# GpSimd adds the identity to two blocks of the loaded slab, in place of TensorE's identity products

## The reference

```python
R = S + eye(N)                     # S is adj
R = R / R.sum(-1)
for n in range(2):                 # two steps
    A  = top_p_attention(Xa, W1, W2, W3)   # softmax over 2048 keys, cut to the top 90% of the mass
    Xf = R @ Xf                    # propagation
    Xa = A @ Xa                    # attention
    Z  = Z + Xf @ U1[n].T + Xa @ U2[n].T
```

## Time and profile before

| | us |
|---|---|
| median of 3 runs | 1008.23 |
| their range | 1007.75 to 1008.57 |
| the profiled execution's own time | 1006.43 |
| its span, first to last instruction | 1004.6 |
| busy: PE, DVE, ACT, POOL | 804.8, 666.2, 474.7, 68.8 |

### The profile page before, as it was taken

How to read it: one execution, slowest core, us unless ns; L and a number is a source line. 1 busy time by engine, 2 the same in 40 slices (tenths; PEclk the granted TensorE clock), 3 DMA queues, 4 the chain that set the end, 5 groups by cost and what they waited for, 6 DMA issues and landing times.

```text
span 1004.6 us, 11941 instructions
## 1 busy us (share of the span) xinstructions
PE 804.8 (80%) x3886; PEld 551.0 (55%) x3886; DVE 666.2 (66%) x2092; ACT 474.7 (47%) x945; POOL 68.8 (7%) x63
## 2 busy tenths in 40 slices
PE   4879984988888865786898788685598999994994
PEld 4844432756666654683575565565295585542342
DVE  5967858488777689734979876788596022245715
ACT  4886334336545556344435646846944241024111
POOL 0020001010000000000000000201001000013001
PEclk9889986988988996989897888899799999997898
DMA  9849502543103100000253300601342819100001
GB/s 336 331 165 432 214 10 84 168 167 126 44 1 125 44 1 2 1 2 0 84 175 117 128 1 1 226 1 53 130 172 70 321 41 427 63 1 0 1 0 42
DMA packets 20219, 108.23 MB, mean 108 GB/s; under 512 B 1824, under 2 KB 8752, under 8 KB 9776
## 3 DMA queue, kind: packets, MB, share of 16 engines
q1 hardware_dynamic: 18752, 106.77, 28.6%
q10 hardware_dynamic: 1392, 0.61, 0.3%
HBM read 88.23 MB, written 19.14 MB: 107 GB/s over the span
## 4 chain that ended last, share of the span: by engine, by line
PE 49%; DVE 25%; ACT 12%; issue 9%; DMA 2%; POOL 1%; DVEq 1%; POOLq 0%; SPq 0%; ACTq 0%
PE PS L802 9%; PE PS L671 6%; DVE AT L1518 6%; PE PS L607 6%; PE PS L541 5%; PE PS L724 4%; PE PS L871 4%; DVE mxv L1657 4%; ACT BC L1243 3%; DVE nd L1521 3%; PE PS L1052 3%; PE PS L1028 3%; ACT AT L1243 3%; DVE AT L2100 3%; PE PS L1058 2%
## 5 line engine op out<-in xcount | busy, mean ns | idle before, releaser
L1074 ACT ACTIVATE AT<-PS 128x512 f32<-128x512 f32 (+2 forms) x240 | 118.7, 559 | 121.3 <-PE PS L541 86.8
L541 PE MATMUL PS<-ident,AT 128*128 128x128 f32 x544 | 85.8, 293 | 38.5 <-DVE rS L2169 18.9
L1657 DVE TENSOR_REDUCE mxv<-PS 128x1 f32<-128x2048 f32 x32 | 73.2, 2288 | 56.7 <-PE PS L724 56.6
L724 PE MATMUL PS<-K,ST 64*128 64x512 f32 x256 | 87.9, 779 | 13.6 <-ACT EA L1211 7.7
L541 PEld LDWEIGHTS PS<-ident,AT 128*128 128x128 f32 x544 | 69.0, 152 | 46.9 <-DVE rS L2169 20.1
L2100 DVE MAX8 AT<-AT 128x8 f32<-128x256 f32 (+2 forms) x336 | 92.7, 347 | 0.7
L802 PE MATMUL PS<-AT 128*128 128x128 f32 x512 | 72.1, 291 | 13.1 <-ACT AT L1074 12.6
L802 PE MATMUL PS<-hr,AT 128*128 128x128 f32 x512 | 71.3, 289 | 8.2 <-ACT AT L1074 7.4
L802 PEld LDWEIGHTS PS<-AT 128*128 128x128 f32 x512 | 65.7, 202 | 21.9 <-ACT AT L1074 17.7
L802 PEld LDWEIGHTS PS<-hr,AT 128*128 128x128 f32 x512 | 65.0, 200 | 17.3 <-ACT AT L1074 11.2
L1074 ACT ACTIVATE ST<-PS 128x512 f32<-128x512 f32 (+3 forms) x43 | 23.9, 561 | 104.6 <-PE PS L1058 24.3
(11 more groups left out here) (297 smaller groups left out, 1370.5 us busy)
## 6 DMA issues: line engine op xcount, KB each, us to landing
AT<-keep_at SPq DMA_DIRECT2D x32, 1024.0 KB, 5.0
EA<-in_adj SPq DMA_DIRECT2D x20, 1024.0 KB, 6.5
keep_at<-AT SPq DMA_DIRECT2D x8, 2048.0 KB, 25.0
AT<-keep_at SPq DMA_DIRECT2D x8, 2048.0 KB, 12.4
AT<-in_adj SPq DMA_DIRECT2D x12, 1024.0 KB, 6.6
EA<-keep_degrees SPq DMA_DIRECT2D x1, 1024.0 KB, 6.5
keep_x<-K SPq DMA_DIRECT2D x4, 256.0 KB, 6.8
out<-EA SPq DMA_DIRECT2D x4, 256.0 KB, 2.3
```

The source lines that it names most:

```text
L541: return pe.transpose(dst, src, ident[0:p, 0:p])
L724: return pe.matmul(bank(to + n), ST[1][half_rows, k * P:(k + 1) * P], keys[half_rows, n * BK:(n + 1) * BK], start=True, stop=True)
L1074: return act.activation(dst, src, ACT.Copy)
L1657: v(dve.tensor_reduce(mxv[:, odd:odd + 1], PS[:, b:b + 4, :], AX.XY, ALU.max))
```

## The change

GpSimd now adds the identity into the slab in SBUF, once it has been loaded: one instruction on two blocks of 128x128, the diagonal blocks of the unit's own two tiles. TensorE's two identity products go. Within each half PE now takes the unit's own tiles (`2*c` and `2*c + 1`, in the first half for `c` below 4, in the second otherwise) last, and waits for a new semaphore `slab_own` ahead of them. POOL does the adds behind the square root of a group: units 0 to 3 behind the root of group 0, 4 and 5 behind that of group 1, 6 and 7 behind that of group 2, and the same in step 1.

```diff
+            def slab_added(u):
+
+                c = u % UNITS
+                pool.wait_ge(slab_in[2 * c // HALF], 16 * (u + 1))
+                here = slab[:, 2 * c:2 * c + 2, :].rearrange("p j (k c) -> p (j k) c", c=P)[:, 0:4:3, :]
+                pool.tensor_tensor(here, here, ident[:, :].unsqueeze(1).to_broadcast([P, 2, P]), ALU.add)\
+                    .then_inc(slab_own, 1)
+
+            SLABS = {0: range(0, 4), 1: range(4, 6), 2: range(6, UNITS),
+                     4: range(UNITS, UNITS + 4), 5: range(UNITS + 4, UNITS + 6), 6: range(UNITS + 6, 2 * UNITS)}
             for gi in range(STEPS * NB):
...
                 pool.tensor_tensor(sZ[:, gi % 2, :], Z[:, gi % 2, :], ex[:, 1, 0:G], ALU.pow).then_inc(root_ok, 1)
+                for u in SLABS.get(gi, ()):
+                    slab_added(u)
...
                 left = hr if p == 0 else Xf
-                for j in range(NT):
-                    if j % HALF == 0:
-                        pe.wait_ge(slab_in[j // HALF], 16 * (u + 1))
-                    mm = pe.matmul(bank(6)[:, 2 * P:4 * P], left[:, j, :], slab[:, j, :],
-                                   start=(j == 0), stop=(j == NT - 1))
-                    if j == HALF - 1:
-                        mm.then_inc(un_half, 1)
-                    if j == 0:
-                        for k in range(2):
-                            pe.matmul(bank(6)[:, (2 + k) * P:(3 + k) * P], left[:, 2 * c + k, :], ident[:, :],
-                                      start=False, stop=False)
-                mm.then_inc(un_half, 1)
+                own = (2 * c, 2 * c + 1)
+                for h in range(2):
+                    pe.wait_ge(slab_in[h], 16 * (u + 1))
+                    tiles = [j for j in range(h * HALF, (h + 1) * HALF) if j not in own]
+                    tiles += [j for j in own if j // HALF == h]
+                    for j in tiles:
+                        if j == own[0]:
+                            pe.wait_ge(slab_own, u + 1)
+                        mm = pe.matmul(bank(6)[:, 2 * P:4 * P], left[:, j, :], slab[:, j, :],
+                                       start=(h == 0 and j == tiles[0]), stop=(h == 1 and j == tiles[-1]))
+                    mm.then_inc(un_half, 1)
```

More of the change, by code:

```diff
@@ L244, in gnn_kernel @@
             sure_steps ksum_ok mean_mm mean_ok lnz_ok gap_ok guess_steps guess_ok
-            cs_ok at_saved un_half un_st un_t un_row un_pr un_z th_ok sum_ok roots_ok fin_sq bias_ok h2_t h2_st hw_mm x2_ok mask_ok
+            cs_ok at_saved un_half slab_own un_st un_t un_row un_pr un_z th_ok sum_ok roots_ok fin_sq bias_ok h2_t h2_st hw_mm x2_ok mask_ok
             ln_steps ln_sq ln_var ln_pow ln_root ln_y ln_t ln_ts ln_x ln_x2 h2_act diag_ok early_in x2_dma"""
@@ L254, in gnn_kernel @@
          ksum_ok, mean_mm, mean_ok, lnz_ok, gap_ok, guess_steps, guess_ok,
-         cs_ok, at_saved, un_half, un_st, un_t, un_row, un_pr, un_z, th_ok, sum_ok, roots_ok, fin_sq, bias_ok, h2_t, h2_st, hw_mm, x2_ok, mask_ok,
+         cs_ok, at_saved, un_half, slab_own, un_st, un_t, un_row, un_pr, un_z, th_ok, sum_ok, roots_ok, fin_sq, bias_ok, h2_t, h2_st, hw_mm, x2_ok, mask_ok,
          ln_steps, ln_sq, ln_var, ln_pow, ln_root, ln_y, ln_t, ln_ts, ln_x, ln_x2, h2_act, diag_ok, early_in, x2_dma) = [sem(n) for n in names.split()]
```

## The result

The changed kernel takes 1002.61 us, the median of 12 runs (995.95 to 1006.02). The kernel before, run beside it, takes 1008.04 us (12 runs, 1003.70 to 1009.15). The ratio is 0.994 with a 95% interval of 0.9916 to 0.9963.

What follows compares the result with a forecast made beforehand. TensorE was taken to bound the kernel only where it ends last, in eight of 16 units. 3.56 us gained less 0.95 of contention gave 2.6 us, so a median of 1005.6 us, range 1003.8 to 1007.8.

Steps and rivals of the forecast that it cites:

- PE's work pays, and only on the chain: TensorE, busy 80% of the span: removing matmuls pays only where PE ends last, in eight of 16 units.
- The rival that all 16 count: Propagation units: all 16 gain as if PE bound everywhere, 7.1 us less contention, 1002.1 us; chance 0.02.
- The chain units are worth 8 x 0.445 = 3.56 us: Units 0, 1, 2, 4, 5, 7, 9, 10: removed products save their high-clock price, 3.56 us; other end 4.37.
- Low price saved in full: Products at the low clock save their full price, small DVE operations get past: 4.0 us, 1004.2 us; chance 0.14.
- What is late next: Where stalls shrink: DVE takes units 0 to 2's gain whole, unit 5's refill moves up, ACT still ends last at 314.54.
- The reordering costs nothing: Diagonal tiles last in their half: moves nothing by itself, cost nothing, bounds -0.1 and +0.1 us.
- PE never waits for POOL: Adds before the diagonal tiles: POOL has 3.2 to 4.2 us, PE waits nothing; at most 1.5 us for one unit.
- An add takes 0.6 us: POOL's add on two blocks: between 0.6 and 2.4 us, taken as 0.6.
- the slower rival: DVE before units 0, 4 and after POOL's step 1 root: 2.4 us adds hold DVE, 3.6 us slower, 1011.9; chance 0.07.
- Contention of 0.38 + 0.38 + 0.19: Adds of units 0, 4 and, by half, 8 delay DVE work on the chain: 0.95 us in all.
- The forecast of the median: Whole kernel: profiled 1003.8 us plus the 1.8 us by which the median exceeded the profiled execution gives 1005.6 us.

Runs made afterwards that it cites:

- matched pair: The traces of the kernel before and of g, side by side, alike up to unit 0; spans 1004.6 and 998.3 us.
- e1: Kernel before without any identity product and without adds, so the identity is missing; 995.87 us (six runs, ratio 0.9895), repeated 1001.32 us (0.9948).
- g: g_chain_only: kernel before without identity products in units 0, 1, 2, 4, 5, 7, 9, 10, no adds; 1000.70 us, 0.994; repeated 1002.32 us.
- h: h_pool_off_path: changed kernel, but units 0, 4, 8 keep PE's identity products and get no add; 999.72 us (0.9944), repeated 1000.60 us (0.9936).
- fill_chain_only: g plus 20 unread identity-by-itself products in PE's waits in the queries of five groups; 1001.01 us, 0.9946.
- fill_after: Changed kernel plus 20 unread identity-by-itself products in PE's waits in the queries of five groups; 1002.52 us, 0.9962.
- filled pair: Kernel before with 20 unread products in PE's waits (1003.46 us, 0.9977) against fill_chain_only; 2.6 +- 1.2 us apart by the means.
- e0_after_again: Changed kernel once more, no edit, for a second trace; 1002.1 us, 0.9947.

## Why the prediction was wrong

1. *PE's work pays, and only on the chain.* Right. The eight units read off the chain give all of the gain, the other eight none that shows (1.0005). The rival that all 16 count named 1002.1 us, close to the 1002.61 measured, by luck: its mechanism would have made the other eight worth 3.6 us, and their interval ends at 2.2.
2. *The chain units are worth 8 x 0.445 = 3.56 us.* This is the term that failed. As work the size is right: 0.44 at unit 1, 1.34 at unit 4, 10.38 us a unit, 3.8 in the matched pair. But the term measured about 6: the kernels without all or most of these products (the changed one, e1, g and h with their repeats: 76 runs, mean 1000.0) lie 5.9 us (+- 0.8) below those with them (168 runs, 1006.0), with the adds' cost inside where there are adds. The step said that where the clock is low "work that is removed before it lets later work slide into the low stretch", on the condition that "the rise comes at the same time after PE starts", and weighed 0.44 against 0.85 for the removed records alone. The condition failed: around unit 4 PE started 1.34 us earlier and the rise came 6.9 us earlier. Of the 1.81 us that unit 4 gained beyond its products' 0.44, 0.41 is L613's own low price; the other 1.40 is L607's, which the step didn't price at all. Neither bound (3.56, 4.37) held this, since both counted only the removed records. The range was too narrow for that reason. With the term at 6 and the contention near 0.85 the sum comes to some 5 us, as measured.
3. *Low price saved in full*, the rival of 4.0 us, has the right direction and the wrong mechanism: 4.0 is still too little.
4. *What is late next.* Half right. Unit 5's refill did move up, and DMA left the chain there, but ACT's copy took its place (243.04), which put unit 4 off the chain, and gave back 1.05 us in the matched pair. This was not in the sum.
5. *The reordering costs nothing.* Not contradicted: 0.9992 (0.9971 to 1.0014), an interval far wider than the 0.1 us of the forecast.
6. *PE never waits for POOL.* Right, in all 16 units.
7. *An add takes 0.6 us.* 0.72 measured, nearly right, and of no weight. The 2.4 of two whole L488 records, on which the slower rival stood, was wrong for the reason given there: most of the record was waiting.
8. *Contention of 0.38 + 0.38 + 0.19.* Measured 0.45 + 0.40 + 0. The first two are confirmed in place and size, the third add ran beside DVE's gap but for its last 0.13 us. The Trainium skill, "SBUF — State Buffer", section "Who interferes with whom", has such a pair exclude each other for the whole instruction. The trace agrees in that the add ended only 0.6 us behind the L1529 inside which it had begun. It doesn't agree in the size: DVE lost 0.40 to 0.45 of the add's 0.72 us, and at unit 8 a two-input DVE operation began before the add's end and took its usual 0.16.
9. *The forecast of the median.* It added 1.8 us, the distance of one profiled execution from the median, to the result. In the changed kernel that distance is nothing (1002.60 and 1002.61). It isn't a constant, but where one execution fell in the spread.

What stays open: why each low stretch begins and ends where it does. The traces show that less work on PE and filled waits move the ends. Without filled waits, unit 4 is out of the low stretch in all seven traces that lack the products of units 0 to 2. But h_pool_off_path, fill_chain_only and fill_after are as fast as the others without products and run unit 4 at the low level, and no run here tells which places bring the gain there. That the clock brings the extra rests on the matched pair, on the granted clocks of all executions and on the fill. The interval of the filled pair (1.4 to 3.8 us, by the means) only just parts from that of g_chain_only against before (3.8 to 8.3 by the ratio, 4.3 to 7.3 by the means).

## What to carry to other kernels

Price removed TensorE work at its duration on the chain of waits, and then look at where the clock is low near it: if a low stretch ends inside matmuls that follow on the chain, work that moves by 1 us can move the clock's rise by several, either way, and the range must hold that. Where a kernel has such stretches, some products that nobody reads in TensorE's waits are a cheap test: if they make it faster, part of a measured gain may be clock and not work. Take twelve runs or more before a difference of 5 us in a thousand is believed.

## What the runs showed of the hardware

- *The spread goes with the clock in the kernel before, less so in the changed one.* Executions of the kernel before lie between 998.70 and 1009.34 us, and where its mean granted clock is 0.899 the time is under 1000, at 0.882 it is about 1009. The first twelve of the changed kernel aren't sorted by it: 995.95 us at 0.892, 1004.17 at 0.897. The changed kernel's profiled execution had unit 0 begin at the low level and lost 2.7 us there (9.86 us, first row of its timeline above); e0_after_again ran the same unit in 7.17. The windows at that place, the changed kernel, then the one before:

```profile
175.00:180.00 5.00, 4.07 (x10) 3.27 (x11) 3.09 (x8) 1.65 (x1) 0.00 (x0) 0.50 0.01 3
```

```profile
175.00:180.00 5.00, 5.00 (x26) 4.46 (x26) 2.10 (x2) 2.06 (x2) 0.00 (x0) 1.00 0.06 10
```

  That the two spans differ by 3.8 us where the medians differ by 5.4 has another reason: the profiled execution of the changed kernel is its median, that of the kernel before (1006.43) lies 1.6 us under its own (1008.04).
- *Twenty useless products made a kernel faster*, by 2.3 us (0.9977, 0.9957 to 0.9997).
- *Not every POOL operation holds DVE up.* In the kernel before a power on POOL ran for 2.90 us, and a two-input DVE operation that started inside it took its usual 0.16:

```profile
160.32 2.90 POOL L458 TENSOR_TENSOR esc<-cs,ex 128x16 f32<-128x16 f32 x1 [25.02 <-DVE cs L1511]
...
162.19 0.16 DVE L1511 TENSOR_TENSOR gs<-gs 128x4 f32<-128x4 f32 x1 [1.86 <-ACT gs L1216]
```

  The add, as long as it is alone, takes 0.72 us and delayed such an operation by 0.40 ahead of unit 4.
